# A conditional residual layer on one core: SP, ACT and DVE streams written out without loops, eight subject numbers to a register load, subject row on sixteen partitions, tiles 0 and 1 stored singly

## What is computed

```
w = weights[subjects]                          # (128, 128, 128)
out = jnp.einsum('bct,bcd->bdt', x, w)
return x + out
```

## Time and profile before

| | us |
|---|---|
| median of three runs | 324.39 |
| the profiled execution's own time | 325.0 |
| its span, first to last instruction | 323.2 |
| PE busy (clock granted 0.93 on average) | 244.7 |
| DVE busy | 196.1 |
| ACT busy | 132.3 |
| bytes moved over the span | 134.80 MB, 417 GB/s on average |

### The profile page before, as it was taken

One profiled execution on the slowest core, in us unless ns is written; L12 is line 12 of the kernel. 1 busy time (PEld: TensorE's weight loads), 2 busy tenths in 40 slices (PEclk: granted clock), 3 DMA queues, 4 the chain that ended last, 5 costly groups with the idle time before them and its releaser, 6 DMA issues.

```text
span 323.2 us, 3584 instructions
## 1 busy us (share of the span) xinstructions
PE 244.7 (76%) x1024; PEld 113.0 (35%) x1024; DVE 196.1 (61%) x261; ACT 132.3 (41%) x131; POOL 0.8 (0%) x7
## 2 busy tenths in 40 slices
PE   0599999788868787666996869868668768698640
PEld 0244444343434333333442334434324323344320
DVE  3278888863766755577184773737765547736360
ACT  4045646632434434244152442424443424424240
POOL 1000000000000000000000000000000000000000
PEclk9999999997989999999697998979999979989785
DMA  8999999999999999999999999999999999999994
GB/s 285 422 420 396 431 424 427 428 424 431 426 428 431 423 431 427 425 431 425 431 429 424 431 426 427 432 423 431 427 425 431 425 430 429 424 431 424 428 430 196
DMA packets 17975, 134.80 MB, mean 417 GB/s; under 512 B 1073, under 2 KB 1586, under 8 KB 1586
## 3 DMA queue, kind: packets, MB, share of 16 engines
q1 hardware_dynamic: 9232, 67.64, 50.0%
q10 hardware_dynamic: 8738, 67.11, 49.1%
HBM read 67.63 MB, written 67.11 MB: 417 GB/s over the span
## 4 chain that ended last, share of the span: by engine, by line
DMA 62%; PE 27%; DVEq 2%; DVE 2%; issue 2%; ACT 1%; ACTq 0%; SPq 0%
DMA out<-x_ring 40%; PE product L211 27%; DMA x_ring<-x 21%; DVEq L123 2%; DMA weight_halves<-weights 1%; DVE x_ring L132 1%; DVE x_ring L131 0%; DVEq L44 0%; ACT weight_bank L160 0%; DVE weight_ring L124 0%; ACT x_ring L169 0%; DVE weight_bank L117 0%; DVEq L124 0%; ACTq L187 0%; SPq L81 0%
## 5 line engine op out<-in xcount | busy, mean ns | idle before, releaser
L211 PE MATMUL product<-x_ring,weight_ring 64*128 64x512 f32 x1024 | 244.7, 632 | 66.3 <-DMA x_ring<-x 49.5
L211 PEld LDWEIGHTS product<-x_ring,weight_ring 64*128 64x128 f32 x1024 | 113.0, 200 | 197.2 <-issue 140.1
L131 DVE TENSOR_TENSOR x_ring<-product,x_ring 64x1024 f32<-64x1024 f32 x64 | 77.9, 1217 | 104.3 <-PE product L211 104.3
L168 ACT COPY x_ring<-product 64x1024 f32<-64x1024 f32 x64 | 64.5, 1008 | 176.3 <-PE product L211 176.3
L132 DVE TENSOR_TENSOR x_ring<-product,x_ring 64x1024 f32<-64x1024 f32 x64 | 78.6, 1228 | 0.8
L169 ACT COPY x_ring<-product 64x1024 f32<-64x1024 f32 x64 | 64.2, 1003 | 0.8
L124 DVE COPY weight_ring<-weight_bank 64x256 f32 x128 | 36.9, 288 | 7.1 <-issue 4.3
L111 DVE COPY weight_bank<-weight_halves 64x1024 f32<-64x1024 f32 x2 | 1.4, 688 | 4.8 <-DMA weight_halves<-weights 4.8
L160 ACT COPY weight_bank<-weight_halves 64x1024 f32<-64x1024 f32 x2 | 2.2, 1123 | 2.3 <-DMA weight_halves<-weights 2.3
L160 ACT ACT_TABLE_LOAD x1 | 1.3, 1283 | 1.4 <-PEq L229 1.4
L117 DVE TENSOR_TENSOR weight_bank<-weight_bank,eye 64x512 f32<-64x512 f32 x2 | 1.4, 687 | 0.3 <-ACT weight_bank L160 0.2
## 6 DMA issues: line engine op xcount, KB each, us to landing
x_ring<-x SPq DMA_DIRECT2D x32, 2048.0 KB, 17.2
out<-x_ring ACTq DMA_DIRECT2D x30, 2048.0 KB, 31.2
out<-x_ring ACTq DMA_DIRECT2D x4, 1024.0 KB, 12.2
weight_halves<-weights SPq DMA_DIRECT2D x1, 512.0 KB, 4.2
subject_row<-subjects ACTq DMA_DIRECT2D x1, 0.5 KB
```

The lines of the kernel that those rows point to most:

```text
L131: dve.tensor_tensor(x_ring[LOW, slot, 0, :], low[LOW, :], x_ring[LOW, slot, 0, :], add)
L168: act.copy(x_ring[LOW, slot, 1, :], low[HIGH, :])
L211: last = pe.matmul(product[slot % PRODUCTS][a][:, cols], weight_ring[half, slot, r, :], x_ring[half, slot, r, cols], start=r == 0, stop=r ...
```

## The change

The subject row is loaded onto 16 partitions in place of one (the same 512 bytes on each). DVE clamps the row once on its first partition to 0..7, and then loads eight subject numbers to registers with one instruction, every fourth tile, without the bounds check. The loops of SP, ACT and DVE are written out. Tiles 0 and 1 are stored singly, as the last four tiles were before; the counts that SP and ACT wait for follow from `stores`. PE's code is as it was.

```
+    SINGLE = (*range(PAIR), *range(TILES - REST, TILES))
+    SUBJECT_ROWS = 16
+    def stores(pairs, place):
+        return sum(PAIR if (pair * PAIR_SLOTS + place) * PAIR in SINGLE else 1 for pair in range(pairs))
...
-        subject_row = ctx.enter_context(nc.sbuf_tensor("subject_row", [1, B], i32))
+        subject_row = ctx.enter_context(nc.sbuf_tensor("subject_row", [SUBJECT_ROWS, B], i32))
...
 SP
-            with sp.Fori(1, LAPS) as lap:
-                for place in range(PAIR_SLOTS):
-                    sp.wait_ge(x_out[place], lap * DMA_INC)
-                    load(lap * PAIR_SLOTS + place, place)
...
+            for pair in range(PAIRS):
+                lap, place = divmod(pair, PAIR_SLOTS)
+                if lap:
+                    sp.wait_ge(x_out[place], stores(lap, place) * DMA_INC)
+                elif place >= LOADS_AHEAD:
+                    sp.wait_ge(x_in[place - LOADS_AHEAD], DMA_INC)
+                sp.dma_start(x_ring[:, place * PAIR:(place + 1) * PAIR, :, :], x_of_pair[pair]).then_inc(x_in[place], DMA_INC)
...
 DVE
-                for a, half in enumerate((LOW, HIGH)):
-                    subject = dve.value_load(subject_row[0:1, bass.ds(tile * 2 + a, 1)], min_val=0, max_val=S - 1)
+            def subjects_of(tile):
+                _, numbers = nc.values_load_multi_w_load_instructions(
+                    subject_row[0:1, tile * 2:(tile + PICK_AHEAD) * 2], engines=(mybir.EngineType.DVE,), min_val=0,
+                    max_val=S - 1, skip_runtime_bounds_check_because="DVE has clamped subject_row to 0 .. S - 1")
+                return numbers
+            def pick(slot, numbers):
+                for subject, half in zip(numbers, (LOW, HIGH)):
                     done = dve.tensor_copy(weight_ring[half, slot, :, :], weight_bank[half, bass.ds(subject, 1), :, :])
...
+            dve.wait_ge(subjects_in, DMA_INC)
+            dve.tensor_scalar(subject_row[0:1, :], subject_row[0:1, :], 0, S - 1, mybir.AluOpType.max,
+                              mybir.AluOpType.min).then_inc(clamped, 1)
...
-            with dve.Fori(0, LAPS) as lap:
+            for tile in range(TILES):
+                sums(tile, tile % SLOTS)
+                ahead = tile + PICK_AHEAD
+                if ahead < TILES:
+                    if ahead % PICK_AHEAD == 0:
+                        numbers = subjects_of(ahead)
...
 ACT
-            act.dma_start(subject_row[0:1, :], subjects.rearrange("(one b) -> one b", one=1)).then_inc(subjects_in, DMA_INC)
+            act.dma_start(subject_row[:, :], subjects.rearrange("(one b) -> one b", one=1).broadcast_to(
+                (SUBJECT_ROWS, B))).then_inc(subjects_in, DMA_INC)
...
+            for tile in range(TILES):
+                slot = tile % SLOTS
+                cross(tile, slot)
+                if tile in SINGLE:
+                    whole(tile)
+                    act.dma_start(out_of_pair[tile // PAIR, :, j, :], x_ring[:, slot, :, :]).then_inc(x_out[place], DMA_INC)
+                elif j == PAIR - 1:
+                    whole(tile)
+                    act.dma_start(out_of_pair[tile // PAIR], x_ring[:, place * PAIR:(place + 1) * PAIR, :, :]).then_inc(
+                        x_out[place], DMA_INC)
```

More of the change, by code:

```diff
@@ L57, in subject_residual_kernel @@
         subjects_in = ctx.enter_context(nc.semaphore("subjects_in"))
+        clamped = ctx.enter_context(nc.semaphore("clamped"))
         weights_in = ctx.enter_context(nc.semaphore("weights_in"))
@@ L79, in _ @@
         def _(sp):
-            def load(pair, place):
-                sp.dma_start(x_ring[:, place * PAIR:(place + 1) * PAIR, :, :],
-                             x_of_pair[bass.ds(pair, 1)]).then_inc(x_in[place], DMA_INC)
             sp.dma_start(weight_halves[:, :, :, :],
                          weights.rearrange("(i a) (h r) d -> (a h) i (r d)", a=2, r=R)).then_inc(weights_in, DMA_INC)
-            for place in range(PAIR_SLOTS):
-                if place >= LOADS_AHEAD:
-                    sp.wait_ge(x_in[place - LOADS_AHEAD], DMA_INC)
-                load(place, place)
-            with sp.Fori(1, LAPS) as lap:
-                for place in range(PAIR_SLOTS):
-                    sp.wait_ge(x_out[place], lap * DMA_INC)
-                    load(lap * PAIR_SLOTS + place, place)
-            for place in range(REST // PAIR):
-                sp.wait_ge(x_out[place], LAPS * DMA_INC)
-                load(LAPS * PAIR_SLOTS + place, place)
+            for pair in range(PAIRS):
[3 more added lines that the diff above has]
+                elif place >= LOADS_AHEAD:
+                    sp.wait_ge(x_in[place - LOADS_AHEAD], DMA_INC)
+                sp.dma_start(x_ring[:, place * PAIR:(place + 1) * PAIR, :, :], x_of_pair[pair]).then_inc(x_in[place], DMA_INC)
         @block.gpsimd
@@ L118, in add_eye @@
                     (H, S, H)), add)
-            def pick(tile, slot):
-                for a, half in enumerate((LOW, HIGH)):
-                    subject = dve.value_load(subject_row[0:1, bass.ds(tile * 2 + a, 1)], min_val=0, max_val=S - 1)
+            def subjects_of(tile):
[5 more added lines that the diff above has]
+                for subject, half in zip(numbers, (LOW, HIGH)):
                     done = dve.tensor_copy(weight_ring[half, slot, :, :], weight_bank[half, bass.ds(subject, 1), :, :])
@@ L144, in _ @@
             dve.wait_ge(eyes_added, 1)
-            dve.wait_ge(subjects_in, DMA_INC)
+            dve.wait_ge(clamped, 1)
+            numbers = subjects_of(0)
             for tile in range(PICK_AHEAD):
-                pick(tile, tile).then_inc(picked, 1)
-            with dve.Fori(0, LAPS) as lap:
[L151 to L155, removed]
+                pick(tile, numbers[tile * 2:tile * 2 + 2]).then_inc(picked, 1)
+            for tile in range(TILES):
[4 more added lines that the diff above has]
+                        numbers = subjects_of(ahead)
+                    own = ahead % PICK_AHEAD * 2
+                    pick(ahead % SLOTS, numbers[own:own + 2])
         @block.scalar
@@ L180, in _ @@
             bank(HIGH, HIGH, ODDS).then_inc(bank_high, 1)
[L181 to L190, removed]
-                place, j = divmod(slot, PAIR)
[L192 to L195, removed]
+            for tile in range(TILES):
+                slot = tile % SLOTS
+                place, j = divmod(slot, PAIR)
+                cross(tile, slot)
[6 more added lines that the diff above has]
+                        x_out[place], DMA_INC)
             for place in reversed(range(PAIR_SLOTS)):
-                act.wait_ge(x_out[place], DMA_INC * (LAPS + (PAIR if place < REST // PAIR else 0)))
+                act.wait_ge(x_out[place], DMA_INC * stores(LAPS + (place < REST // PAIR), place))
         @block.tensor
```

## The result

The changed kernel takes 323.66 us (median of 14 runs, 323.20 to 324.18) against 324.56 us (14 runs, 323.90 to 324.94). The ratio is 0.9974, with a 95% interval of 0.9968 to 0.9981: faster by 0.26%, or 0.84 us. In a second set of runs on another occasion it was 0.9982 (0.9973 to 0.9991), so 0.6 to 0.9 us is what the two medians give, and the intervals together run from 0.3 to 1.0 us. The forecast was 323.8, a gain of 0.57 us.

A forecast was written before the change was run, and what follows sets the result against it. The 16 DMA engines, never idle at 427 GB/s, were taken as the bound, one ending late. Hole -0.54, rate with earlier stores -0.05, more descriptors +0.02 gave -0.57 us: 323.8 us, range 322.9 to 325.2.

The forecast's parts named there:

- the hole: DMA rate dip behind the first store, 26 to 28 us; laid to ACT's queue's first use; 0.54 us gained.
- E: Rival: the last DMA engine is less late through fewer register loads or code laps; 1.0 us more gained, 322.8; chance 0.12.
- the prediction's own signs: Between 20 and 30 us: no window under 400 GB/s confirms the hole's gain; one near 300 means it stays.
- B: Rival: the hole behind the first store stays, only earlier, at about 22 to 24 us; 324.4 us; chance 0.24.
- SP's first hole and its harmless restart: SP's queue: 76 and 113 GB/s at 2.0 to 3.0 us on first use; its later restart lost only 0.06 us.
- The count of packets: Profile page: 1104 packets under 512 B expected if the subject row on 16 partitions runs on 16 engines.
- The load of eight: DVE's start: eight numbers per instruction replace four loads; PE starts 0.7 us earlier, bounds 1.3 earlier to 1.6 later.
- Loops and register instructions cost nothing: SP, ACT and DVE: removed register instructions and checks lie beside waits for DMA; worth nothing.
- Longer texts: DVE's and ACT's longer code brings two to four more code packets over the DMA engines; taken as 0.
- Rival C: Two more code packets fall on the DMA engine that ends last; 326.3 us, or 325.1 with 8 KB packets; chance 0.12.
- Rival D: At the end: a last load over 2.3 us later lays the tail bare; 324.8 to 325.8 us; chance 0.10.
- the ring's share: Earlier stores share the ring's bytes with loads, so the last load lands later by at most 4.3 us.

The follow-up runs named there:

- row1: The changed kernel with the subject row on one partition again; 323.78 us, ratio 0.9983 to the kernel before.
- pair_first: The changed kernel with tiles 0 and 1 stored as one pair; 323.89 us, ratio 0.9983 to the kernel before.
- before_row16: The kernel before with only the subject row put on 16 partitions; 324.69 us, ratio 1.0001.
- again: The changed kernel, unchanged, run and profiled a second time; 323.97 us, ratio 0.9982 to the kernel before.
- one_number_loads: The changed kernel, loops written out, with one register load and its checks per number, 128 in all; 325.88 us, ratio 1.0044 to the kernel before.
- padded: The changed kernel with four more DVE instructions per tile that only raise an idle semaphore; 325.28 us, ratio 1.0024 to the kernel before.

## Why the prediction was right, and where it was right for another reason

**The time** was right: 323.8 forecast, 323.66 measured. That the sum came out is luck. Its one large term, 0.54 us for the hole, is worth nothing that the runs can tell, and what the two pairs of traces show in its place, a last engine 0.9 us less late, stood in the sum at nothing and among the rivals as E.

**The hole's term** was mis-sized and its mechanism wrong. It stood at 0.54 us gained; the trace gives 0.27, and its undoing (row1, pair_first) and its doing alone (before_row16) move the time by nothing that the runs can tell. By the prediction's own signs (no window under 400, against one near 300) the window of 311 GB/s speaks for B. I took SP's first hole and its harmless restart as evidence for the first use of a queue. That was a misreading: I had the DMA engines busy throughout, but in the second window the share was 0.45, so they were idle for half of it. The evidence for rival B, that no engine was spared in the hole, was the better one. I also priced the loss one to one, as if the last engine had its share of it; no run shows that it has.

**The count of packets** was right: 1104 expected, 1105 (with the code packet of 40 bytes) and in "again" 1104, so the row on 16 partitions does run on 16 engines. The rule of the Trainium skill, page "DMA: Bandwidth & Descriptors", section "Why a DMA increments its semaphore by 16 and not by 1", on the number of engines held.

**The load of eight** was mis-sized. PE started at 10.39 for 12.07, 1.7 us earlier, where I had 0.7 and a bound of 1.3. The row of the changed kernel:

```profile
L124 DVEq TENSOR_LOAD <-subject_row x16: 601/796/1576, 7.8 to 277.2; - x16
```

Eight registers cost twice one, not eight times. I had also left out the checks that went with each load. With one number to a load and no loops (one_number_loads) PE starts at 11.64. The first store was issued at 19.04 (19.6 forecast); stores land in 26.2 us and loads in 22.0 (27 and 20 forecast).

**Loops and register instructions cost nothing** was right on the compute engines, which wait as before. It was incomplete, since what goes with them seems to be part of the last DMA engine's lag; that is not shown.

**Longer texts.** Two to four more code packets were expected; of 8 KiB there were two, in both traces. Zero was nearly right, by a smaller margin than I thought. In the first trace the engine that brings DVE's code ends last, at 320.60 us, 0.24 us behind the sloping one (320.36); in "again" the sloping one ends last, at 321.27, and DVE's code costs nothing. Rival C was the right mechanism: it costs 1.4 us in padded and, by the steps, seems to be most of the 1.9 us in one_number_loads. Its price of 0.6 to 1.9 us a packet is 0.84 to 0.92 us for most packets of 8 KiB, and 0.55 for one of them in each trace. The Trainium skill, page "Runtime: NRT & Kernel Launch", section "Instruction fetch mechanics", says that the fetches of a long text are mostly hidden. For a DMA engine that is never idle these traces show otherwise, by those 0.84 to 0.92 us.

**Rival D** did not happen here (the last load was 0.6 us later, 2.3 were to spare), but did in one_number_loads, brought about by a late engine and not by the ring's share.

**Rival E** is what the traces show most of: 1.3 of the 1.6 us between the first two profiled executions, 0.9 of 1.2 us on average over both pairs. I gave it 0.12. Of its supposed causes the register loads are excluded; why the engine is less late is open.

## What to carry to other kernels

When all DMA engines are busy to the end, the kernel's time is that of the latest of them: read the last five windows of a microsecond, count how many engines' worth of rate is left, and price an edit by what it does to that one. Writing out a loop is not free there, since 8 KiB of text hold one DMA engine up by 0.55 to 0.92 us, and for DVE's text it was the same one each time; keep the text short, with several register values to a load. A loss of rate early in the stream, of up to 0.42 us in the sum over all engines, did not show in the time; why not is open.

## What was not expected of the hardware

Amid full traffic a code packet of 8 KiB delays its DMA engine by 0.84 to 0.92 us as a rule, of which the packet itself is 0.31 us (26.7 GB/s); in each trace one of them, ahead of 93 us, costs 0.55 (0.69 in before_row16). One DMA engine is slower than the other 15 by 0.07 to 0.13 us in each 9.8 us, 0.7 to 1.3%, in all 14 traces, with no register loads in the kernel too. One load of eight registers takes 0.80 us in the middle, against 0.39 for one.
